# Cross-attention with an expert layer: logits first in every half, and the second norm's wide operations behind the next half's probabilities

## The reference

```
lat  = layer_norm(layernorm(x));  kv_in = [layer_norm(ctx), lat]          # 128 rows per batch
q = lat @ Wq;  k = kv_in @ Wk;  v = kv_in @ Wv                            # 16 heads of 64
alphas = softmax(mask(q k^T / 8));  x = x + (alphas v) @ Wo
z = layernorm(x)                                                          # the second norm
gates: sigmoid(z @ gate_w), the best 2 of 8, scaled to sum 1
out = x + shared(z) + sum_e gate_e * (silu(z @ w1_e) * (z @ w3_e)) @ w2_e # 8 experts of width 64
```

## Time and profile before

| what | us or share |
|---|---|
| profiled execution, its own time | 1191.51 |
| its span | 1189.8 |
| PE busy | 1142.1 (96%) |
| PE weight loads busy | 1087.4 (91%) |
| VectorE busy | 905.7 (76%) |
| ScalarE busy | 900.2 (76%) |
| GpSimd busy | 670.1 (56%) |
| probabilities on GpSimd (L419), 256 | 266.9, 1043 ns each |
| exponentials on ScalarE (L523), 1024 | 402.2, 413 ns each |

### The profile page before, as it was taken

How to read it: one execution, slowest core, us unless ns; L and a number is a source line. 1 busy time by engine, 2 the same in 40 slices (tenths; PEclk the granted TensorE clock), 3 DMA queues, 4 the chain that set the end, 5 groups by cost and what they waited for, 6 DMA issues and landing times.

```text
span 1189.8 us, 29786 instructions
## 1 busy us (share of the span) xinstructions
PE 1142.1 (96%) x9000; PEld 1087.4 (91%) x9000; DVE 905.7 (76%) x4095; ACT 900.2 (76%) x3180; POOL 670.1 (56%) x781
## 2 busy tenths in 40 slices
PE   6899999999999999999999999999999999999986
PEld 5899999999999999999999999999999999999976
DVE  4777787777787777787778787778787778777776
ACT  4988777777777877777877778777778777777761
POOL 5565565665565665555665555665656565656431
PEclk9999999999999999999999999999999999999999
DMA  6001110111110111011111001111001111001101
GB/s 162 19 10 37 31 30 24 42 41 42 27 33 25 42 41 42 24 29 31 42 42 42 19 24 42 42 41 42 20 24 42 42 42 41 20 23 28 28 23 33
DMA packets 64399, 42.61 MB, mean 36 GB/s; under 512 B 8944, under 2 KB 63856, under 8 KB 64240
## 3 DMA queue, kind: packets, MB, share of 16 engines
q1 hardware_dynamic: 63056, 39.66, 12.7%
q10 hardware_dynamic: 1184, 1.05, 0.3%
HBM read 36.25 MB, written 4.45 MB: 34 GB/s over the span
## 4 chain that ended last, share of the span: by engine, by line
PE 76%; POOL 9%; DVE 7%; issue 4%; ACT 3%; DMA 1%; SPq 0%; DVEq 0%; ACTq 0%; POOLq 0%
PE bank L788 15%; PE bank L790 15%; PE bank L789 15%; PE bank L850 14%; PE bank L830 9%; PE bank L794 5%; POOL probs L419 3%; DVE pT_lo L679 2%; POOL x_r L441 2%; POOL x L448 2%; ACT pT_hi L496 2%; PE bank L859 2%; POOL x L444 2%; DVE x L699 1%; PE bank L907 1%
## 5 line engine op out<-in xcount | busy, mean ns | idle before, releaser
L419 POOL TENSOR_TENSOR probs<-probs,rdenom 128x512 f32<-128x512 f32 x256 | 266.9, 1043 | 340.8 <-DVE rdenom L654 340.8
L523 ACT ACTIVATE probs<-logits,neg_max 128x128 f32<-128x128 f32 x1024 | 402.2, 413 | 0.5 <-DVE neg_max L646 0.5
L850 PEld LDWEIGHTS bank<-kvT,tT 128*128 128x128 f32 x2048 | 267.3, 191 | 22.3
L850 PE MATMUL bank<-kvT,tT 128*128 128x128 f32 x2048 | 269.3, 274 | 0.0
L679 DVE TENSOR_TENSOR pT_lo<-bank,pT_hi 128x512 fp32r<-128x512 f32 x256 | 175.2, 685 | 90.6 <-ACT pT_hi L496 82.7
L646 DVE CUSTOM_DVE_ANT_0 logits<-bank,mask_add 128x128 f32<-128x128 f32 x1024 | 232.3, 282 | 5.1 <-PE bank L850 4.9
L496 ACT CAST pT_hi<-bank 128x512 fp32r<-128x512 f32 x256 | 152.9, 597 | 80.9 <-PE bank L830 80.4
L523 ACT ACTIVATION_READ_ACCUMULATOR probs<-logits,neg_max 128x1 f32 x1024 | 213.3, 208 | 0.0
L483 ACT ACTIVATE h_tanh<-bank 128x256 f32<-128x256 f32 x160 | 61.3, 383 | 170.3 <-PE bank L790 164.0
L689 DVE TENSOR_TENSOR cT_lo<-bank,cT_hi 128x512 fp32r<-128x512 f32 x256 | 174.7, 682 | 0.3
L830 PE MATMUL bank<-ident,probs 128*128 128x128 f32 x1024 | 155.7, 275 | 20.0 <-POOL probs L419 20.0
(11 more groups left out here) (111 smaller groups left out, 2610.2 us busy)
## 6 DMA issues: line engine op xcount, KB each, us to landing
gates<-gates_dram SPq DMA_DIRECT2D x62, 256.0 KB, 4.1
kv_raw<-in_ctx SPq DMA_DIRECT2D x32, 128.0 KB, 2.8
kv_raw<-in_x SPq DMA_DIRECT2D x32, 128.0 KB, 2.8
mask_raw<-in_mask_BxS_ik SPq DMA_DIRECT2D x32, 128.0 KB, 3.5
x_res<-in_x SPq DMA_DIRECT2D x32, 128.0 KB, 3.2
out<-out_sb SPq DMA_DIRECT2D x32, 128.0 KB, 1.8
gates_dram<-g_denseT SPq DMA_DIRECT2D x124, 2.0 KB
wq_raw<-in_L_xattn_Wq SPq DMA_DIRECT2D x1, 512.0 KB, 4.9
```

The costliest lines, as they stand in the source:

```text
L419: nc.gpsimd.tensor_tensor(probs[n][:, :, :], probs[n][:, :, :], rdenom[n][:, :].unsqueeze(2).broadcast_to([P, PAIRS, P]), ALU.mult).then_i ...
L523: nc.scalar.activation(probs[n % 4][:, r, :], logits[n % 2][:, r, :], ACT.Exp, bias=neg_max[n % 2][:, r:r + 1], scale=-1.0, accum_out=deno ...
L850: last = nc.tensor.matmul(S_ps[k % 2][:, P * r:P * (r + 1)], tT[:, k % 4, hd:hd + 2, :], kvT[p][:, k % 4, :], start=True, stop=True)
```

## The change

On PE the logits of a half come before the transposition of the probabilities and the values, in every half. The transposition of x2 is moved from the end of half 0 to half 1, behind the values. On GpSimd the two wide operations of the second norm (now the function `center`) are taken out of half 7 and put into half 0 of the next frame, behind the probabilities of that half; x_ve and x_r stay in half 7. In the last group (i = 32) `center` is called at once, as before. The waits go along with their instructions; ScalarE's, VectorE's and SyncE's programs are the same. Nothing is added or left out.

```diff
                     nc.gpsimd.tensor_tensor(kv_lo[par][:, :, :], kv_f[:, :, :], kv_hi[par][:, :, :].bitcast(fp32),
                                             ALU.subtract).then_inc(kv_step, 1)
 
+            def center(i):
+
+                step = X2_STEPS * (i - 1)
+                after(pool, x2T_in_psum, i - 1)
+                nc.gpsimd.tensor_tensor(x2[:, :, :], x1_of(i)[:, :, :],
+                                        x1_mv[:, :, 0].unsqueeze(2).broadcast_to([P, TT, D]),
+                                        ALU.subtract).then_inc(x2_step, 1)
+                pool.wait_ge(x2_step, step + 3)
+                nc.gpsimd.tensor_tensor(x2[:, :, :], x2[:, :, :], x1_r[:, :].unsqueeze(2).broadcast_to([P, TT, D]),
+                                        ALU.mult).then_inc(x2_step, 1)
+
             def frame(j, p):
                 i = 2 * j + p
                 for k in range(HALVES):
...
                         for r in (0, 1) if k == 2 else (2, 3):
                             nc.gpsimd.tensor_tensor(h[1 - p][:, r, :], h[1 - p][:, r, :], gates[:, r, :],
                                                     ALU.mult).then_inc(h_routed_done, 1)
+                    if k == 0 and has(j, p, 2, NG):
+                        center(i - 1)
                     if has(j, p, -1, NG - 2):
                         keys(j, p + 1, {0: (5,), 1: (6,), 4: (7,), 5: (8,)}.get(k, ()))
                     if has(j, p, -2, NG - 3):
...
                         pool.wait_ge(x2_step, step + 1)
                         nc.gpsimd.tensor_tensor(x1_r[:, :], x1_ve[:, :], minus_half[:, 0:TT],
                                                 ALU.pow).then_inc(x2_step, 1)
-                        after(pool, x2T_in_psum, i - 1)
-                        nc.gpsimd.tensor_tensor(x2[:, :, :], x1_of(i)[:, :, :],
-                                                x1_mv[:, :, 0].unsqueeze(2).broadcast_to([P, TT, D]),
-                                                ALU.subtract).then_inc(x2_step, 1)
-                        pool.wait_ge(x2_step, step + 3)
-                        nc.gpsimd.tensor_tensor(x2[:, :, :], x2[:, :, :], x1_r[:, :].unsqueeze(2).broadcast_to([P, TT, D]),
-                                                ALU.mult).then_inc(x2_step, 1)
+                        if i == NG:
+                            center(i)
 
             frames(pool, frame)
 
...
                     if k == 7 and has(j, p, 3, NG):
                         expert_outputs(p, 1).then_inc(y_in_psum, 1)
 
-                    if has_half(j, p, k, 3):
-                        pe.wait_ge(probs_ready, e - 2)
-                        after(pe, pT_lo_ready, e - 3)
-                        for r in range(PAIRS):
-                            last = nc.tensor.transpose(PT_ps[:, P * r:P * (r + 1)], probs[(k - 3) % 4][:, r, :], ident[:, :])
-                        last.then_inc(pT_in_psum, 1)
-
-                    if has_half(j, p, k, 4):
-                        kl, par = half_buffers(p, k, 4)
-                        pe.wait_ge(pT_lo_ready, e - 3)
-                        if kl == 0:
-                            pe.wait_ge(kv_step, KV_STEPS * (i + 1))
-                        after(pe, cT_lo_ready, e - 4)
-                        matmul3(C_ps[:, :], kv_hi[par][:, kl % 4, :], kv_lo[par][:, kl % 4, :], pT_hi[kl % 2][:, :],
-                                pT_lo[kl % 2][:, :]).then_inc(C_in_psum, 1)
-
                     if has_half(j, p, k, 0):
                         if k == 0:
                             pe.wait_ge(kvT_ready, i + 1)
...
                             last = nc.tensor.matmul(S_ps[k % 2][:, P * r:P * (r + 1)], tT[:, k % 4, hd:hd + 2, :],
                                                     kvT[p][:, k % 4, :], start=True, stop=True)
                         last.then_inc(S_in_psum, 1)
+
+                    if has_half(j, p, k, 3):
+                        pe.wait_ge(probs_ready, e - 2)
+                        after(pe, pT_lo_ready, e - 3)
+                        for r in range(PAIRS):
+                            last = nc.tensor.transpose(PT_ps[:, P * r:P * (r + 1)], probs[(k - 3) % 4][:, r, :], ident[:, :])
+                        last.then_inc(pT_in_psum, 1)
+
+                    if has_half(j, p, k, 4):
+                        kl, par = half_buffers(p, k, 4)
+                        pe.wait_ge(pT_lo_ready, e - 3)
+                        if kl == 0:
+                            pe.wait_ge(kv_step, KV_STEPS * (i + 1))
+                        after(pe, cT_lo_ready, e - 4)
+                        matmul3(C_ps[:, :], kv_hi[par][:, kl % 4, :], kv_lo[par][:, kl % 4, :], pT_hi[kl % 2][:, :],
+                                pT_lo[kl % 2][:, :]).then_inc(C_in_psum, 1)
+
+                    if k == 1 and has(j, p, 2, NG + 1):
+                        pe.wait_ge(x2_step, X2_STEPS * (i - 1))
+                        for t in range(TT):
+                            last = nc.tensor.transpose(X_ps[:, P * t:P * (t + 1)], x2[:, t, :], ident[:, :])
+                        last.then_inc(x2T_in_psum, 1)
                     if k == 2 and has(j, p, -1, NG - 2):
 
                         pe.wait_ge(kv_step, KV_STEPS * (i + 1) + 6)
...
                                 pe.wait_ge(attnT_ready, NG)
                             last_outputs(p, k - 4)
 
-                    if k == 0 and has(j, p, 2, NG + 1):
-                        pe.wait_ge(x2_step, X2_STEPS * (i - 1))
-                        for t in range(TT):
-                            last = nc.tensor.transpose(X_ps[:, P * t:P * (t + 1)], x2[:, t, :], ident[:, :])
-                        last.then_inc(x2T_in_psum, 1)
 
             frames(pe, frame)
 
```

More of the change, by code:

```diff
@@ L824, in frame @@
                         expert_outputs(p, 1).then_inc(y_in_psum, 1)
+                    if has_half(j, p, k, 0):
+                        if k == 0:
+                            pe.wait_ge(kvT_ready, i + 1)
+                        if k in (0, 4):
+                            pe.wait_ge(t_ready, e + 4)
+                        after(pe, logits_ready, PAIRS * (e - 1))
+                        for r in range(PAIRS):
+                            hd = 8 * (k // 4) + 2 * r
+                            last = nc.tensor.matmul(S_ps[k % 2][:, P * r:P * (r + 1)], tT[:, k % 4, hd:hd + 2, :],
+                                                    kvT[p][:, k % 4, :], start=True, stop=True)
+                        last.then_inc(S_in_psum, 1)
                     if has_half(j, p, k, 3):
```

## The result

The changed kernel takes 1219.88 us (median, 1218.44 to 1220.1) against 1192.26 (1191.34 to 1194.49) for the kernel before, measured beside it: ratio 1.0226, 95% interval 1.0209 to 1.0244. It is slower by 27.6 us; 28.4 was forecast.

The account below looks back on a forecast made before the run. PE was taken to bound the kernel, busy 35.18 of 35.84 us a frame. Four new waits on ScalarE, +60.0, less 31.6 for removed waits, gave +28.4 on 1191.5: 1219.9, 1220 us, range 1200 to 1233.

Parts of the forecast that it names:

- A: The forecast itself: four new waits of PE on ScalarE, timed from P, a half's first weight load; +28 us, chance 0.62.
- Half 2: The keys' transposition on PE waits behind ScalarE's g_exp: +0.82 us in 29 frames, 23.8 us.
- Half 6: PE's attention output transposition waits behind ScalarE's attnT: +0.50 us in 30 frames, 0.9 in frame 31, 15.9 us.
- Half 0: PE's query chunk waits behind ScalarE's tT, delayed from half 7 (start P7): +0.22 us in 31 frames, 6.8 us.
- Half 1: PE's gate matmuls wait behind x2T, x2T_hi and x2T_lo: +0.45 us in 30 frames, 13.5 us.
- What goes: PE's waits for GpSimd, 0.80 at the probabilities' transposition and 0.19 at x2's, vanish: 29.7 us; with the first frame, 31.6.
- Halves 3, 4, 5 and 7 at nothing: Query work after the values covers ScalarE's later copies in these halves: cost nothing; 3 us if one fails by 0.1.
- The start, -1.5: First frame: four waits of the probabilities' transposition for GpSimd shrink by 0 to 3.3 us; 1.5 taken.
- B: Rival: only half 2's wait shows, PE's own work absorbs halves 0, 1 and 6; -8, 1184 us; chance 0.10.
- C: Rival: loads pulled past waits make each wait about 0.11 us shorter; 13 less, 1207 us; chance 0.12.
- D: Rival: new neighbours on PE cost 0.05 us a half; 13 more, 1233 us; chance 0.08.
- E: Rival: GpSimd's probabilities of half 0 late again, 24 us of their transposition's wait stay; 1243 us; chance 0.05.

Follow-up runs that it names:

- e3: Changed kernel with g_exp on ScalarE moved ahead of the copies pT_hi and cT_hi in half 2; 1192.38 us, ratio 0.9996.
- e6: Changed kernel with the logits behind the values again in half 2 alone; 1198.4 us, ratio 1.0041.
- e4: Changed kernel with attnT on ScalarE moved ahead of the copies pT_hi and cT_hi in half 6; 1204.71 us, ratio 1.0105.
- e12: Changed kernel with the logits behind the values again in half 7 alone; 1212.62 us, ratio 1.0171.
- e2: Changed kernel with the logits behind the values again in every half, GpSimd's split and x2's transposition in half 1 kept; 1168.96 us, ratio 0.9794.
- e11: Changed kernel with the logits behind the values again in half 1 alone; 1227.51 us, ratio 1.029.
- e9: Kernel before with only g_exp on ScalarE moved ahead of the copies; 1193.65 us, ratio 1.0003.
- e5: e2 with g_exp on ScalarE moved ahead of the copies; 1167.35 us, ratio 0.9778.
- e10: e5 with the logits first in half 4 alone; 1158.87 us, ratio 0.9718.

## Why the prediction was right, step by step

**The price of the order (A).** Right. The four positions came out within 0.03 us of the forecast: L873 at P + 3.14 (3.17 forecast), L910 at P + 3.26 (3.25), the gate matmuls at P + 4.09 (4.09), the chunk at P7 + 4.99 (594.10 - 589.11; 4.99). They could be worked out because the earlier trace rows show the same chains in the last frames, where ScalarE already waits for PE.

**Half 2.** Mechanism shown by e3 and e6. The term was 0.82 a frame and is 0.75; e6 gives 21.5 us for 23.8 forecast. What was a little off is above all what such a pause absorbs: 0.12 taken, 0.20 shown by e3 against the changed kernel. The wait itself is 1.23 for 1.27 (3.14 less 1.91), and what before lost in this half is 0.28 for 0.33 (4.88 less e3's 4.60), which offset each other.

**Half 6.** +0.47 for +0.50; e4 gives 15.2 for 15.9. **Half 0.** +0.04 for +0.03; e12 gives 7.3 for 6.8. **Half 1.** -0.31 for -0.35 (0.45 less 0.80; the working's own 4.09 less 3.62 is 0.47, which would make -0.33 and 0.6 us more in the sum).

**What goes.** The 0.80 and the 0.19 went, as e2 shows (23.9 us, a frame of 35.04 for 35.84; most of the other 0.19 is given back at the gate matmuls, whose load there follows the one before it by 0.25 where 0.11 is normal). That the cover of the probabilities would be thin was right too: 0.35 here, and with 0.9 less of it (e11) 0.53 of wait.

**Halves 3, 4, 5 and 7 at nothing.** Nearly: +0.05 a frame in 3 to 5, 1.5 us in all: 4.15, 4.85 and 4.84 before, 4.16, 4.87 and 4.86 after. It has no wait beside it in the list, and each is near the 0.01 in which the rows are read; where it comes from is open.

**The start, -1.5: missed.** The first load of the attention output's transposition came at 74.43 before and at 75.87 after, +1.44, where -1.0 was forecast (-1.5, and half 6's 0.5 once). The keys' transposition of the first frame is ahead of the first reordered instruction. Its load stands at 30.83 before and here after:

```profile
32.58 0.47 PEld L873 LDWEIGHTS bank<-ident,kv_f 128*128 128x128 f32 x4
```

So 1.75 us were lost where both kernels do the same. 0.94 of it was there at the keys' transposition before that (19.17 and 20.11). The rest, 0.81, is nearly all TensorE's clock, in the columns of the earlier trace rows, before and then after:

```profile
20.00:25.00 5.00, 3.69 (x18) 3.69 (x19) 2.16 (x11) 1.90 (x4) 2.08 (x3) 0.66 0.18 52
25.00:30.00 5.00, 5.00 (x42) 4.83 (x42) 2.11 (x12) 3.16 (x9) 4.08 (x4) 1.00 0.19 52
```

```profile
20.00:25.00 5.00, 3.40 (x16) 3.10 (x17) 2.22 (x12) 1.45 (x3) 1.14 (x2) 0.56 0.15 37
25.00:30.00 5.00, 4.94 (x33) 4.77 (x32) 0.38 (x3) 2.35 (x4) 4.69 (x5) 0.76 0.23 68
```

Behind a wait of 1.7 us for VectorE (1.8 after) the granted clock is 0.50, the level of 1.2 GHz, from 21.5 to 24.6 before and from 22.5 to 27.3 after, and the loads follow each other by 0.21; then it is 1.00 and they follow by 0.12. This does not go with the order: e9, with PE's order of before, stands at 32.42 with 0.55 and 0.77, and e4, with the new order, at 30.97 with 0.66 and 1.00. It belongs to the single execution. From the keys' transposition to the attention output's it is 43.60 before and 43.29 after: -0.3, where -1.0 was forecast. There L830's waits fell by more than the 1.5, from 3.4 to 1.3 us, but new waits came: 0.4 behind attnT, which the sum had, and 0.8 behind tT and 1.0 ahead of the logits, which it had at nothing for this frame. These are what the step had wrong.

The end was nearly right: 0.7 less, where 0.4 less was forecast for the serial stretch and 0.2 more for the last half 0. From 74.4 to 1142.84 before, 1068.4, it is 1096.2 after, +27.7, where the sum had 29.6 (60.0, less 0.5 for the first half 6, 0.2 for the last half 0, and the 29.7 that go). With +1.44 and -0.7 that is the 28.5 of the span. So that span and forecast agree to 0.1 us is luck: the frames came to 1.9 less, the start to 2.4 more and the end to 0.5 less. The mechanism is right frame by frame, +0.97 for +1.00; the medians, 27.6 us apart, confirm the size only to about 2 us (95% interval of the ratio: 24.9 to 29.1 us).

**The rivals.** B needed three waits absorbed by PE's own work; all three stood. It also had on its side the advice of the Trainium skill (Perfetto Trace Analysis, Optimization Strategy: find the gaps of the most contended engine and let what they wait for start sooner). Of e2 that held, 23.9 us for a wait of 0.99 a frame. Of e9 it did not: 0.33 a frame taken out, ratio 1.0003. C: L873's load stood with its wait at 603.88, 0.12 behind g_exp's end, and no wait came out a load shorter: no load was pulled past a wait here. What the Trainium skill says (TensorE: Matmul & The Clock Gate, Step-by-step: what each phase is for) is of loads pulled ahead of matmuls in flight, and these rows do not contradict it; to carry it over to a group that waits was the prediction's own step. D wanted 0.05 in every half; halves 7, 3, 4 and 5, which have the new neighbours and no other new term, changed by 0.04 together, 0.01 each, and half 0 came out 0.01 above its own terms. E: the 3.0 us of L850 refute it. F: 1.0226. The chances of A, C, D and E add to 0.87, not to the 0.85 given for slower.

## What to carry to other kernels

An order of work on one engine that costs nothing there can still move every result that the next engine's queue handles in order; before reordering, list for each consumer what stands behind the moved result in its queue and which of that the first engine asks for next. Often the cheaper edit is on the consumer: here a 0.2 us instruction that depended on none of its predecessors, put ahead of them, was worth as much as the whole change cost. And where a wait is removed in a frame that several engines share, look for the resource with the next-smallest slack first: in e5 and e9 the wait taken away brought no gain clear of noise, and with the next one moved too 8.5 us came (e10 against e5).

## What the runs showed of the hardware

- PE's "busy" rose from 1142.1 to 1153.8 us and from 35.18 to 35.52 a frame for identical work at the same granted clock, while its weight loads' fell from 1087.4 to 1082.4. Part of a wait seems to be counted as a matmul's time: at L873 the weight loads stand idle for 36.6 us and the matmuls beside them for 24.7. So busy PE is no measure of the work here; the distances between weight loads are.
- Behind a pause of 1.26 us in front of a transposition PE came to the next half 0.20 sooner than without it (2.49 against 2.69, e3). A wait is thus worth less than its length.
- "issue" stood for a wait on another engine in the three large cases that come once a frame: ScalarE's g_exp (36.6 us in 29), VectorE's x2T_lo (10.9 in 30) and cT_lo (8.7 in 32).
